# The query-times-key-bias term of plain attention: a row sum on VectorE in place of one-column matmuls

## Chip, cores and metric

One core of one Trainium2 chip. The metric is the device time in microseconds of one execution of the whole program. TensorE runs the matmuls, VectorE (DVE) reductions and elementwise work, ScalarE (ACT) activations, GpSimd (POOL) and SyncE (SP) mostly issue DMAs here.

## What is computed

The program is a stack of four blocks, each with an attention-like and a feed-forward part. The change lies in block 1's attention, "plain attention", over 8 sequences of 112 latent rows with 375 context rows each, all of width 1024:

```python
def _L1_xattn_ref(text, features, Wq, bq, Wk, bk):
    Q = jnp.einsum('btx,dx->btd', text, Wq) + bq
    K = jnp.einsum('bpx,dx->bpd', features, Wk) + bk
    scale = 1.0 / jnp.sqrt(jnp.asarray(K.shape[-1], K.dtype))
    scores = jnp.einsum('btd,bpd->btp', Q, K) * scale
    attn = jax.nn.softmax(scores, axis=-1)
    return jnp.einsum('btp,bpd->btd', attn, features)
...
x = x + jnp.tanh(g_xattn[1]) * _L1_xattn_ref(_layernorm(x, axis=-1), ctx_4096, ...)
```

A score is Q·(features Wk) plus Q·bk. The second term is one number per row of Q, the same for all 375 context rows.

## The kernel before

Plain attention handles the 8 sequences in 4 pairs. PE, VectorE and ScalarE run pairs 0 to 2 in a hardware loop and pair 3 as separate code (`every_pair`, L397). Everything is float32; each matmul of the code becomes two matmul instructions with two weight loads.

TensorE's order in a pair is written out by hand: the query projection of both sequences (L776, `projected("qT", ...)`, into PSUM banks 2, 3, 6, 7), the key projection of Q (L776, `projected("tT", ...)`, banks 0, 1, 4, 5), and then for each sequence s the scores (L792, 8 matmuls of 375 columns) followed by 8 matmuls of one column with the key bias (L795), which put Q·bk into column 400 of the same bank. Then come the transposes of the probabilities of sequence 0 (L807), the transposes of the next pair's normed rows z (L673), those of the probabilities of sequence 1, and the output products (L815).

VectorE does two unlike things. Beside the attention it sorts distances for a nearest-neighbour search that a later block needs: `points.begin` (L500) releases ScalarE's squares, and three sorts per sequence (L521 to L531) follow, each waiting for its squares; the first sort of a sequence also waits until the ranks of the sequence before are stored. Between the sorts of sequence 0 and those of sequence 1 it norms the next pair's rows z in place (L442 to L465). After all sorts it takes up the scores: copy of Q·bk (L915), row maximum (L916), L919 and L921, which release ScalarE's exponential (L870). At the end of a pair it scales the output products and adds them to x (L938).

ScalarE copies qT and tT out of PSUM, does the squares, stores the ranks, takes the norm's roots (in its queue ahead of the squares of sequence 1 and of the copies of tT) and the exponentials. SP loads z of the next pair into the same buffer when its rows have been turned (`zT_ready`), then stores and loads x. POOL loads the biases, the points (a megabyte per sequence, broadcast to all partitions) and the context.

Of the kernel before, what the change touches and what calls it, by code (L numbers as in the profile page):

```python
# [402 lines left out]

def stream_ahead(sp, x, z, x_in, x_out, x_loaded, z_loaded, x_done, x_stored, z_used, at_last):


    for s in range(2):
        sp.dma_start(x[:, s, :], x_in[s]).then_inc(x_loaded[s], 16)

    def pair(p, last):  # L410
        if not last:
            for s in range(2):
                sp.wait_ge(*z_used(s, p))
                sp.dma_start(z[:, s, :], x_in[p * 2 + (s + 2)]).then_inc(z_loaded[s], 16)
        else:
            at_last()
        for s in range(2):

            sp.wait_ge(x_done, p * 2 + (s + 1))
            sp.dma_start(x_out[p * 2 + s], x[:, s, :]).then_inc(x_stored[s], 16)  # L420

            sp.wait_ge(x_stored[s], p * 16 + 16)
            if not last:
                sp.dma_start(x[:, s, :], x_in[p * 2 + (s + 2)]).then_inc(x_loaded[s], 16)

    every_pair(sp, pair)
# [271 lines left out]
def plain_attention(nc, C, banks, gate, x_in, x_out, A, nearest, early, ahead, rise):  # L698
# [4 lines left out]
    with ExitStack() as ctx:  # L703
# [8 lines left out]
        nmax, rsum, coef = (s_.sb(n, [Q, 2, 1]) for n in ("nmax", "rsum", "coef"))  # L712
        qbk, total = s_.sb("qbk", [Q, 2, 1]), s_.sb("total", [Q, 2, 1])
        points = Nearest(s_, [5, 6, 7], 2, nearest, A)
# [8 lines left out]
        max_ready, probs_ready, pT_ready, x_done = (  # L723
            s_.sem(n) for n in ("max_ready", "probs_ready", "pT_ready", "x_done"))

        rows_turned = [(("zT", s, h), 4 * s + h) for s in range(2) for h in range(2)]
        scored = [(("qT", i), (2, 3, 6, 7)[i]) for i in range(4)] + [(("tT", i), (0, 1, 4, 5)[i]) for i in range(4)]
        scored += [((st, s, 0), 4 * s + b0) for st, b0 in (("S", 2), ("pT", 3)) for s in range(2)]
        result = [(("o", s, h), 4 * s + h) for s in range(2) for h in range(2)]
        first = Turns(banks, rows_turned, 1)  # L730
        turns = Turns(banks, scored + rows_turned + result, PAIRS - 1)
        final = Turns(banks, scored + result, 1)
# [3 lines left out]
        def _(sp):  # L736
            def ahead_loads():
# [3 lines left out]
            stream_ahead(sp, x, z, x_in, x_out, x_loaded, z_loaded, x_done, x_stored,  # L741
                         lambda s, p: (zT_ready, p * 2 + (s + 1)), ahead_loads)

        @block.gpsimd
        def _(pool):
            pool.dma_start(bq[:], A["L1_xattn_bq"]).then_inc(b_loaded, 16)
            pool.dma_start(bk[:], A["L1_xattn_bk"]).then_inc(b_loaded, 16)
            with pool.Fori(0, PAIRS) as p:
                for s in range(2):
# [8 lines left out]
        def _(pe):  # L758
            pe.wait_ge(wq_loaded, 16)
            for s in range(2):  # L760
                pe.wait_ge(z_ready, s + 1)
                turn_rows(pe, C, first, z[:, s], "zT", s, 0)

            def pair(p, last):
# [16 lines left out]
                pe.wait_ge(zT_ready, p * 2 + 2)  # L781
                projected("qT", wq, zT, None)
                pe.wait_ge(wk_loaded, 16)
                pe.wait_ge(b_loaded, 32)
                projected("tT", wk, qT, qT_ready)
                for s in range(2):
# [4 lines left out]
                    for k in range(KC):  # L791
                        pe.matmul(now.tile(t)[0:Q, 0:CTX], tT[:, s, k, :], cT[:, s, k, :], start=(k == 0), stop=(k == KC - 1))  # L792

                    for k in range(KC):
                        mm = pe.matmul(now.tile(t)[0:Q, 400:401], qT[:, s, k, :], bk[:, k:k + 1], start=(k == 0),  # L795
                                       stop=(k == KC - 1))
                    mm.then_inc(now.full(t), 1)
# [20 lines left out]

            every_pair(pe, pair)

# [65 lines left out]
        def _(dve):  # L886
            for s in range(2):
                dve.sem_inc(ctx_free[s], 1)
            points.credits(dve)
            norm.in_place(dve, z, z_loaded, 0, z_ready)  # L890

            def pair(p, last):
# [3 lines left out]
                for s in range(2):  # L896
                    for i in range(3):
                        points.sort(dve, p * 2 + s, s, i, (3 * s + i) % 2)
                    if s == 0 and not last:
                        norm.in_place(dve, z, z_loaded, p + 1, z_ready)  # L900
                    if s == 0 and last:
                        for b in range(2):
# [9 lines left out]
                for s in range(2):  # L912
                    t = ("S", s, 0)
                    dve.wait_ge(now.full(t), now.count(t, turn))
                    dve.tensor_copy(qbk[:, s, :], now.tile(t)[0:Q, 400:401])  # L915
                    dve.tensor_reduce(nmax[:, s, :], now.tile(t)[0:Q, 0:CTX], AX, ALU.max, negate=True)  # L916
                    dve.drain()

                    dve.tensor_tensor(total[:, s, :], nmax[:, s, :], qbk[:, s, :], ALU.subtract)  # L919
                    dve.drain()  # L920
                    dve.tensor_scalar(nmax[:, s, :], total[:, s, :], qbk[:, s, :], SCALE, ALU.add, ALU.mult).then_inc(max_ready, 1)  # L921
                for s in range(2):
# [19 lines left out]

            every_pair(dve, pair)

# [2250 lines left out]
def layout(a):  # L3195
# [29 lines left out]
    out["L3_lora_AT"] = out.pop("L3_ffn_lora_A").reshape(512, D).T  # L3225
    out["L3_lora_BT"] = out.pop("L3_ffn_lora_B").transpose(0, 2, 1).reshape(512, D)
    for name in ("L1_xattn_bq", "L1_xattn_bk", "L1_ffn_bu1", "L1_ffn_Wu2"):
        out[name] = a[name].reshape(-1, P).T
# [71 lines left out]
```

## Time and profile before

| what | us |
|---|---|
| median of 3 runs | 2813.17 |
| lowest and highest run | 2810.91, 2819.49 |
| span of the profiled execution | 2820.8 |
| TensorE busy in it | 2583.5 |
| VectorE busy in it | 1907.7 |
| ScalarE busy in it | 1080.2 |

Plain attention takes the stretch from about 968 to 1289 us of the span. The profile shows one execution of the program; busy time counts work, not waiting; the granted clock (PEclk) is TensorE's, 1.00 being 2.4 GHz and 0.50 being 1.2 GHz.

### The profile page before, as it was taken

Reading aid. Unit: us, or ns where it says so; the run is one execution under the profiler, and the core shown is the slowest. Engines: PE = TensorE matmul, PEld = TensorE weight load, DVE = VectorE, ACT = ScalarE, POOL = GpSimd, SP = SyncE. Lnnn points to the kernel's source line nnn. Section 1 sums busy time; section 2 is a strip of 40 time slices with the busy share of each in tenths; the row PEclk is TensorE's granted clock in tenths of the full one; section 3 lists DMA queues with packets and bytes.
Section 4 is the critical chain, followed back from the end, with each engine's and each line's share of the span. In section 5 each row is a group of like instructions: output and inputs, shape, how many; then the busy total and the mean of one; then the engine's idle time right before and its main releaser. Section 6 shows DMA issues by size and latency. Waiting matters only on the chain. (4 is left out here: it accounts for less than half of the span.)

```text
span 2820.8 us, 48283 instructions
## 1 busy us (share of the span) xinstructions
PE 2583.5 (92%) x18264; PEld 1842.1 (65%) x18268; DVE 1907.7 (68%) x3366; ACT 1080.2 (38%) x2605; POOL 564.3 (20%) x602
## 2 busy tenths in 40 slices
PE   7999999999999699998899999998688999868888
PEld 5856855855865388885555555555487788556664
DVE  6376376366467677774578877777558889867774
ACT  3443434334345233332334444443255655302222
POOL 0110100001011300000045454455123334200000
PEclk9999999999999899997899999998799999989999
DMA  8011010111110745556275666544240010544421
GB/s 325 2 38 59 1 59 23 38 35 47 38 60 32 255 112 149 145 160 218 111 238 168 176 172 172 166 133 113 71 186 9 24 46 24 140 143 170 168 96 39
DMA packets 154483, 307.64 MB, mean 109 GB/s; under 512 B 84000, under 2 KB 107200, under 8 KB 144760
## 3 DMA queue, kind: packets, MB, share of 16 engines
q1 hardware_dynamic: 128952, 232.78, 25.6%
q0 software_dynamic: 19376, 57.15, 6.6%
q10 hardware_dynamic: 5936, 14.75, 1.8%
q8 instruction: 141, 2.31, 0.3%
q14 instruction: 78, 0.64, 0.1%
HBM read 249.53 MB, written 42.52 MB: 104 GB/s over the span
## 5 line engine op out<-in xcount | busy, mean ns | idle before, releaser
L1758 DVE TENSOR_REDUCE latent_nmax<-bank 112x1 f32<-112x487 f32 x128 | 85.0, 666 | 242.3 <-PE bank L1561 235.9
L1458 POOL TENSOR_SCALAR latent_probs<-latent_probs,latent_rsum 112x487 f32<-112x487 f32 x128 | 88.1, 688 | 789.6 <-DVE latent_rsum L1763 789.6
L2190 POOL TENSOR_SCALAR grouped_probs<-grouped_probs,grouped_rsum 112x375 f32<-112x375 f32 x256 | 169.6, 680 | 279.4 <-DVE grouped_rsum L2246 279.4
L2457 PE MATMUL bank<-ffn_qT,gather_whole 128*128 128x128 bf16 x3584 | 207.1, 220 | 16.7 <-ACT ffn_us L2580 6.7
L2457 PEld LDWEIGHTS bank<-ffn_qT,gather_whole 128*128 128x128 fp8e4 x3584 | 203.1, 98 | 21.7 <-issue 20.5
L2640 POOL TENSOR_TENSOR ffn_h<-ffn_sl,ffn_us 128x512 f32<-128x512 f32 x56 | 127.4, 2275 | 278.0 <-ACTq L2583 278.0
L2137 ACT ACTIVATE grouped_probs<-bank,grouped_nmax 112x375 f32<-112x375 f32 x256 | 143.3, 573 | 76.4 <-DVE grouped_nmax L2242 76.3
L2242 DVE TENSOR_REDUCE grouped_nmax<-bank 112x1 f32<-112x375 f32 x256 | 122.3, 540 | 72.2 <-PE bank L2048 69.9
L2940 PEld LDWEIGHTS bank<-gather_part,points_onehot 123*128 123x128 bf16 x3072 | 111.9, 103 | 63.1 <-DVE points_onehot L3088 32.6
L2184 POOL TENSOR_SCALAR grouped_raw<-grouped_raw,grouped_rscale 128x1024 f32<-128x1024 f32 x96 | 120.5, 1274 | 144.3 <-DVEq L2220 144.2
L2057 PEld LDWEIGHTS bank<-const_ident,grouped_probs 112*125 112x125 f32 x768 | 105.1, 196 | 67.4 <-DVE grouped_probsT L2254 28.8
L1508 PE MATMUL bank<-latent_zT,front_wq 128*128 128x224 f32 x768 | 148.0, 353 | 0.0
L1533 PE MATMUL bank<-latent_wo,latent_oT 128*128 128x512 f32 x336 | 146.6, 592 | 0.0
L1508 PEld LDWEIGHTS bank<-latent_zT,front_wq 128*128 128x128 f32 x768 | 145.0, 190 | 1.9 <-issue 1.8
L2940 PE MATMUL bank<-gather_part,points_onehot 123*128 123x63 bf16 x3072 | 117.5, 200 | 30.0 <-DVE points_onehot L3088 26.3
L2057 PE MATMUL bank<-const_ident,grouped_probs 112*125 112x112 f32 x768 | 109.8, 282 | 24.8 <-DVE grouped_probsT L2254 18.8
L1468 PE MATMUL bank<-front_wkv,front_cT 128*125 128x384 f32 x384 | 127.0, 491 | 0.0
L1468 PE MATMUL bank<-front_cT,front_wkv 128*128 128x375 f32 x384 | 123.3, 478 | 0.0
L1693 ACT ACTIVATE latent_probs<-bank,latent_nmax 112x487 f32<-112x487 f32 x128 | 85.5, 668 | 89.9 <-DVE latent_nmax L1758 82.4
L2573 ACT ACTIVATE ffn_sl<-ffn_gs,ffn_sgu 128x128 f32<-128x128 f32 x224 | 71.6, 390 | 116.5 <-DVEq L2703 116.1
L1520 PE MATMUL bank<-latent_probsT,latent_v 125*96 125x224 f32 (+1 forms) x512 | 110.2, 358 | 4.1 <-DVEq L1777 4.1
L1533 PEld LDWEIGHTS bank<-latent_wo,latent_oT 128*128 128x128 f32 x336 | 63.2, 190 | 73.9 <-issue 73.7
(435 smaller groups left out, 5576.0 us busy)
## 6 DMA issues: line engine op xcount, KB each, us to landing
grouped_raw<-L_weights SPq DMA_DIRECT2D x24, 2048.0 KB, 9.0
points_spread<-numbers SPq DMA_DIRECT2D x16, 912.0 KB
codes<-grouped_flip SPq DMA_DIRECT2D x24, 512.0 KB, 2.6
front_cT<-ctxT SPq DMA_DIRECT2D x8, 1500.0 KB, 6.8
plain_ctxT<-ctxT POOLq DMA_DIRECT2D x8, 1500.0 KB, 22.5
plain_ctx<-ctx POOLq DMA_DIRECT2D x8, 1500.0 KB, 23.4
grouped_ctx<-ctxT SPq DMA_DIRECT2D x8, 1500.0 KB, 6.7
gather_whole<-numbers SPq DMA_DIRECT2D x12, 912.0 KB
```

The costliest lines, as they stand in the source:

```text
L1468: mm = pe.matmul(turns.tile(t)[0:m, 0:n], lhsT(k), rhs(k), start=(k == 0), stop=(k == KC - 1))
L1508: mm = pe.matmul(turns.tile(t)[:, c * 2 * Q:(c + 1) * 2 * Q], wq[:, k, (2 * i + c) * P:(2 * i + c + 1) * P], zT[:, k].rearrange("p s q -> ...
L1520: mm = pe.matmul(turns.tile(t)[0:HD, 2 * half * Q:2 * (half + 1) * Q], v[0:n, k, g * HD:(g + 1) * HD], pT[0:n, half, k], start=(k == 0), s ...
L1533: mm = pe.matmul(turns.tile(t)[:], oT[:, (b - 1) % 2, k, :], wo[:, k, i * 512:(i + 1) * 512], start=(k == 0), stop=(k == OC - 1))
L2057: mm = pe.transpose(turns.tile(t)[0:CT, j * Q:(j + 1) * Q], pr[:, g % 2, j, k * CT:(k + 1) * CT], C.ident[0:Q, 0:Q])
L2137: act.activation(pr[:, i, j, :], turns.tile(t)[0:Q, 0:CTX], ACT.Exp, bias=nmax[:, i, j:j + 1], accum_out=rsum[:, i, j:j + 1]).then_inc(tur ...
L2184: pool.tensor_scalar(w, w, rscale[:, slot, i % m:i % m + 1], MAGIC, ALU.mult, ALU.add).then_inc(raw_scaled, 1)
L2190: pool.tensor_scalar(pr[:, g % 2, j, :], pr[:, g % 2, j, :], rsum[:, g % 2, j:j + 1], 1.0, ALU.mult, ALU.mult)\
L2242: dve.tensor_reduce(nmax[:, g % 2, j:j + 1], turns.tile(t)[0:Q, 0:CTX], AX, ALU.max, negate=True).then_inc(max_ready, 1)
L2457: mm = pe.matmul(ahead.tile(t)[:, i * P:(i + 1) * P], wgu[:, u0 + f // 4, c:c + 2 * P - 1:2], qT[:, k, :], start=(k == 0), stop=(k == KC - 1))
L2640: pool.tensor_tensor(h[:, G * j:G * j + G, :], sl[:, j % 2], us[:, j % 2], ALU.mult).then_inc(h_ready, 1)
L2940: mm = pe.matmul(turns.tile(t)[:, j * RA:(j + 1) * RA], onehot[0:ROWS, u % 3, j * P:(j + 1) * P], part[n][0:ROWS, b % 2, :], start=(n == 0 ...
```

## The change

Q·bk of a row is z·(Wq bk) + bq·bk, z being the normed row. The vector Wq bk is formed once, at the start of the stage: VectorE multiplies each of the 8 row blocks of Wq with a broadcast row of bk, summing along the row (`tensor_tensor_reduce`), and sums bq times bk. In pair 0, between its two projections, TensorE spreads the result over all partitions by 9 matmuls with the identity, into banks 0, 1 and 4; VectorE reads them after its sorts of sequence 0 (`keys_spread`). From then on, for each pair, VectorE multiplies the normed rows with the spread vector and sums along the row (`summed`), right behind the norm; for pair 0 right behind `keys_spread`. The one-column matmuls L795 and the copy L915 are gone. SP loads the next z only after `summed` has read the old one. The loops of TensorE and VectorE over the pairs are unrolled; those of ScalarE, POOL and SP are kept.

```diff
             for s in range(2):
                 sp.wait_ge(*z_used(s, p))
+                sp.wait_ge(*z_summed(s, p))
                 sp.dma_start(z[:, s, :], x_in[p * 2 + (s + 2)]).then_inc(z_loaded[s], 16)
...
             pool.dma_start(bk[:], A["L1_xattn_bk"]).then_inc(b_loaded, 16)
+            pool.dma_start(key_row, rows(A["L1_xattn_bk_row"], P)).then_inc(key_row_loaded, 16)
...
+            def keys_spread():
+                pe.wait_ge(products_ready, 1)
+                for i in range(3):
+                    t = ("keys", i)
+                    pe.wait_ge(spread.free(t), spread.count(t, 0))
+                    for j in range(4 if i < 2 else 1):
+                        k = 4 * i + j
+                        mm = pe.matmul(spread.tile(t)[0:Q, j * P:(j + 1) * P], key_products[:, k:k + 1].broadcast_to([P, Q]), C.ident[:],
+                                       start=True, stop=True)
+                    mm.then_inc(spread.full(t), 1)
...
                 projected("qT", wq, zT, None)
+                if p == 0:
+                    keys_spread()
                 pe.wait_ge(wk_loaded, 16)
-                pe.wait_ge(b_loaded, 32)
                 projected("tT", wk, qT, qT_ready)
...
                     for k in range(KC):
-                        pe.matmul(now.tile(t)[0:Q, 0:CTX], tT[:, s, k, :], cT[:, s, k, :], start=(k == 0), stop=(k == KC - 1))
-
-                    for k in range(KC):
-                        mm = pe.matmul(now.tile(t)[0:Q, 400:401], qT[:, s, k, :], bk[:, k:k + 1], start=(k == 0),
-                                       stop=(k == KC - 1))
+                        mm = pe.matmul(now.tile(t)[0:Q, 0:CTX], tT[:, s, k, :], cT[:, s, k, :], start=(k == 0), stop=(k == KC - 1))
...
-            every_pair(pe, pair)
+            for p in range(PAIRS):
+                pair(p, p == PAIRS - 1)
...
             norm.in_place(dve, z, z_loaded, 0, z_ready)
+            dve.wait_ge(b_loaded, 32)
+            dve.wait_ge(wq_loaded, 16)
+            dve.wait_ge(key_row_loaded, 16)
+            for k in range(KC):
+                dve.tensor_tensor_reduce(out=row_product, in0=wq[:, k, :], in1=key_row, scale=1.0, scalar=0.0, op0=ALU.mult, op1=ALU.add,
+                                         accum_out=key_products[:, k:k + 1])
+                dve.drain()
+            dve.tensor_tensor(bk[:], bk[:], bq[:], ALU.mult)
+            dve.drain()
+            dve.tensor_reduce(key_products[:, KC:KC + 1], bk[:], AX, ALU.add)
+            dve.drain().then_inc(products_ready, 1)
+
+            def keys_spread():
+                for i in range(3):
+                    t = ("keys", i)
+                    dve.wait_ge(spread.full(t), spread.count(t, 0))
+                    if i < 2:
+                        op = dve.tensor_copy(spread_keys[:, i * 512:(i + 1) * 512], spread.tile(t)[0:Q, :])
+                    else:
+                        op = dve.tensor_reduce(key_products[0:Q, KC + 1:KC + 2], spread.tile(t)[0:Q, 0:P], AX, ALU.add)
+                    op.then_inc(spread.free(t), 1)
+                dve.drain()
+
+            def summed(p):
+                for s in range(2):
+                    dve.tensor_tensor_reduce(out=z_product, in0=z[:, s, :], in1=spread_keys[:], scale=1.0, scalar=0.0, op0=ALU.mult, op1=ALU.add,
+                                             accum_out=qbk[:, p % 2, s, :])
+                    dve.drain()
+                    dve.tensor_tensor(qbk[:, p % 2, s, :], qbk[:, p % 2, s, :], key_products[0:Q, KC + 1:KC + 2], ALU.add).then_inc(qbk_ready, 1)
+                dve.drain()
...
                         points.sort(dve, p * 2 + s, s, i, (3 * s + i) % 2)
+                    if s == 0 and p == 0:
+                        keys_spread()
+                        summed(0)
                     if s == 0 and not last:
                         norm.in_place(dve, z, z_loaded, p + 1, z_ready)
+                        dve.drain()
+                        summed(p + 1)
...
-                    dve.tensor_copy(qbk[:, s, :], now.tile(t)[0:Q, 400:401])
                     dve.tensor_reduce(nmax[:, s, :], now.tile(t)[0:Q, 0:CTX], AX, ALU.max, negate=True)
...
-            every_pair(dve, pair)
+            for p in range(PAIRS):
+                pair(p, p == PAIRS - 1)
```

## Rows read from the trace of the kernel before

**Rows 1.** Pair 1, busy time: start:end, length, each engine, granted clock, DMA, GB/s.
```profile
1058.60:1134.30 75.70, 74.66 (x367) 63.60 (x366) 56.59 (x86) 25.85 (x41) 6.67 (x8) 1.00 0.52 146
```

**Rows 2.** TensorE in order of time, pair 0: start, length, line, operation, count.
```profile
1007.09 24.38 PE L776 MATMUL bank<-plain_qT,plain_wk 128*128 128x224 f32 x128
...
1037.52 1.64 PE L795 MATMUL bank<-plain_bk,plain_qT 128*112 128x1 f32 x16
1039.02 5.29 PE L792 MATMUL bank<-plain_ctxT,plain_tT 128*112 128x375 f32 x16
...
1045.65 0.56 PE L807 MATMUL bank<-const_ident,plain_probs 112*125 112x112 f32 x3
```

**Rows 3.** VectorE in order of time, pair 0; in brackets the idle time before.
```profile
976.08 0.82 DVE L465 TENSOR_SCALAR plain_z<-plain_z,plain_ln_mv 112x1024 f32<-112x1024 f32 x1
980.40 0.18 DVE L500 TENSOR_SCALAR plain_here<-plain_here 128x16 f32<-128x16 f32 x1 [3.50 <-DMA plain_here<-points]
...
984.30 1.23 DVE L521 SCALAR_TENSOR_TENSOR plain_near_far<-plain_near_far 128x1024 f32<-128x1024 f32 x1 [0.22 <-ACT plain_near_far L510]
...
1008.42 1.29 DVE L442 BATCH_NORM_STATS2 plain_ln_stats<-plain_z 112x6 f32<-112x512 f32 x2 [0.40 <-issue]
...
1016.80 1.23 DVE L521 SCALAR_TENSOR_TENSOR plain_near_far<-plain_near_far 128x1024 f32<-128x1024 f32 x1 [2.89 <-DMA nearest<-plain_rank]
...
1040.82 0.16 DVE L915 COPY plain_qbk<-bank 112x1 f32<-112x1 f32 x1 [0.38 <-issue]
```

**Rows 4.** Groups of the stage's instructions: count, busy us and mean ns, idle before.
```profile
L521 DVE SCALAR_TENSOR_TENSOR plain_near_far<-plain_near_far 128x1024 f32<-128x1024 f32 x24 | 29.4, 1225 | 21.7 <-ACT plain_near_far L510 10.5 <-DMA nearest<-plain_rank 8.6 <-issue 2.1
...
L465 DVE TENSOR_SCALAR plain_z<-plain_z,plain_ln_mv 112x1024 f32<-112x1024 f32 x8 | 6.5, 814 | 0.6
...
L927 DVE COPY plain_probsT<-bank 125x336 f32<-125x336 f32 x8 | 4.0, 503 | 2.6 <-PE bank L807 2.6
```

**Rows 5.** The tile z (`plain_z`): its loads from issue to landing.
```profile
DMA to landing us min/median/max: 4.4/11.8/14.4
```

**Rows 6.** TensorE in order of time, pairs 1, 2 and 3.
```profile
1121.37 0.56 PE L807 MATMUL bank<-const_ident,plain_probs 112*125 112x112 f32 x3
...
1124.01 10.46 PE L815 MATMUL bank<-plain_ctx,plain_probsT 125*112 125x512 f32 x24
...
1198.21 0.57 PE L807 MATMUL bank<-const_ident,plain_probs 112*125 112x112 f32 x3 [0.98 <-ACTq L873]
...
1274.95 0.58 PE L807 MATMUL bank<-const_ident,plain_probs 112*125 112x112 f32 x3 [1.05 <-ACTq L873]
...
1276.77 11.69 PE L815 MATMUL bank<-plain_ctx,plain_probsT 125*112 125x512 f32 x24
```

**Rows 7.** VectorE in order of time, pairs 1, 2 and 3.
```profile
1060.30 0.25 DVE L500 TENSOR_SCALAR plain_here<-plain_here 128x16 f32<-128x16 f32 x2 [0.75 <-issue]
...
1118.29 0.16 DVE L915 COPY plain_qbk<-bank 112x1 f32<-112x1 f32 x1 [0.38 <-issue]
...
1172.13 1.23 DVE L521 SCALAR_TENSOR_TENSOR plain_near_far<-plain_near_far 128x1024 f32<-128x1024 f32 x1 [2.69 <-DMA nearest<-plain_rank]
...
1196.14 0.16 DVE L915 COPY plain_qbk<-bank 112x1 f32<-112x1 f32 x1 [0.38 <-issue]
...
1212.53 0.25 DVE L500 TENSOR_SCALAR plain_here<-plain_here 128x16 f32<-128x16 f32 x2 [0.40 <-issue]
...
1214.96 1.23 DVE L521 SCALAR_TENSOR_TENSOR plain_near_far<-plain_near_far 128x1024 f32<-128x1024 f32 x1 [2.18 <-ACT plain_near_far L510]
...
1238.78 1.29 DVE L138 BATCH_NORM_STATS2 mem_stats<-mem_x 128x6 f32<-128x512 f32 x2 [0.30 <-issue]
```

**Rows 8.** Three short stretches: columns as in the first group.
```profile
976.00:986.00 10.00, 9.22 (x33) 8.40 (x34) 2.80 (x5) 5.65 (x7) 2.68 (x3) 0.52 1.01 352
...
1020.00:1024.00 4.00, 4.00 (x23) 4.00 (x22) 3.85 (x6) 0.01 (x1) 0.00 (x0) 1.00 0.32 133
...
1276.00:1278.00 2.00, 2.00 (x5) 1.39 (x6) 1.09 (x5) 0.00 (x0) 0.00 (x0) 0.50 0.06 12
```

More of the change, by code:

```diff
@@ L401, in every_pair, with stream_ahead @@
     pair(PAIRS - 1, True)
-def stream_ahead(sp, x, z, x_in, x_out, x_loaded, z_loaded, x_done, x_stored, z_used, at_last):
+def stream_ahead(sp, x, z, x_in, x_out, x_loaded, z_loaded, x_done, x_stored, z_used, at_last, z_summed):
     for s in range(2):
@@ L712, in plain_attention @@
         nmax, rsum, coef = (s_.sb(n, [Q, 2, 1]) for n in ("nmax", "rsum", "coef"))
-        qbk, total = s_.sb("qbk", [Q, 2, 1]), s_.sb("total", [Q, 2, 1])
+        qbk, total = s_.sb("qbk", [Q, 2, 2, 1]), s_.sb("total", [Q, 2, 1])
+        spread_keys, key_products = s_.sb("spread_keys", [Q, D]), s_.sb("key_products", [P, KC + 2])
+        flat_t, flat_p = tT[:].rearrange("p s k q -> p (s k q)"), pr[:].rearrange("q s n -> q (s n)")
+        key_row, row_product, z_product = flat_t[:, 0:D], flat_t[:, D:D + D // 2].bitcast(BF16), flat_p[:, 0:D // 2].bitcast(BF16)
         points = Nearest(s_, [5, 6, 7], 2, nearest, A)
@@ L724, in plain_attention @@
             s_.sem(n) for n in ("max_ready", "probs_ready", "pT_ready", "x_done"))
+        key_row_loaded, products_ready, qbk_ready = (s_.sem(n) for n in ("key_row_loaded", "products_ready", "qbk_ready"))
         rows_turned = [(("zT", s, h), 4 * s + h) for s in range(2) for h in range(2)]
@@ L730, in plain_attention @@
         first = Turns(banks, rows_turned, 1)
+        spread = Turns(banks, [(("keys", i), (0, 1, 4)[i]) for i in range(3)], 1)
         turns = Turns(banks, scored + rows_turned + result, PAIRS - 1)
@@ L741, in _ @@
             stream_ahead(sp, x, z, x_in, x_out, x_loaded, z_loaded, x_done, x_stored,
-                         lambda s, p: (zT_ready, p * 2 + (s + 1)), ahead_loads)
+                         lambda s, p: (zT_ready, p * 2 + (s + 1)), ahead_loads, lambda s, p: (qbk_ready, p * 2 + (s + 1)))
         @block.gpsimd
@@ L914, in pair @@
                     dve.wait_ge(now.full(t), now.count(t, turn))
-                    dve.tensor_copy(qbk[:, s, :], now.tile(t)[0:Q, 400:401])
                     dve.tensor_reduce(nmax[:, s, :], now.tile(t)[0:Q, 0:CTX], AX, ALU.max, negate=True)
                     dve.drain()
-                    dve.tensor_tensor(total[:, s, :], nmax[:, s, :], qbk[:, s, :], ALU.subtract)
+                    dve.tensor_tensor(total[:, s, :], nmax[:, s, :], qbk[:, p % 2, s, :], ALU.subtract)
                     dve.drain()
-                    dve.tensor_scalar(nmax[:, s, :], total[:, s, :], qbk[:, s, :], SCALE, ALU.add, ALU.mult).then_inc(max_ready, 1)
+                    dve.tensor_scalar(nmax[:, s, :], total[:, s, :], qbk[:, p % 2, s, :], SCALE, ALU.add, ALU.mult).then_inc(max_ready, 1)
                 for s in range(2):
@@ L3226, in layout @@
     out["L3_lora_BT"] = out.pop("L3_ffn_lora_B").transpose(0, 2, 1).reshape(512, D)
+    out["L1_xattn_bk_row"] = a["L1_xattn_bk"]
     for name in ("L1_xattn_bq", "L1_xattn_bk", "L1_ffn_bu1", "L1_ffn_Wu2"):
```

## The prediction, made before the kernel was run
> **What bounds the kernel now.** I read the trace in this order: the grouped stretches of the plain-attention stage, then TensorE's order of time, then VectorE's, then the costs of single operations.
>
> One pair of the stage lasts 75.70 us, and TensorE has work in 74.66 of them, VectorE in 56.59 [rows 1]. That looks like a stage bound by TensorE, with a quarter of VectorE's time to spare. The order of time says otherwise. In pair 0 TensorE finishes the second score block (its last one-column products included) and starts the first transposes of the probabilities at 1045.65 without a pause [rows 2], while VectorE reaches its first work on the scores (L915) only at 1040.82, straight from sorting [rows 3]. The road from there to these transposes is the copy, the maximum, two small operations and ScalarE's exponential. Pair 2 gives its length: VectorE starts at 1196.14 [rows 7] and TensorE, having waited 0.98 us, starts at 1198.21 [rows 6], so 2.07 us. By that, pair 0 could not have transposed before 1042.89, a slack of 2.8 us against 1045.65; pair 1 (1118.29 + 2.07 = 1120.36 against 1121.37, [rows 6, 7]) has 1.0 us; pairs 2 and 3 have none, since TensorE itself waits about 1 us there (0.98 and 1.05, [rows 6]). So both engines are bounds, within 3 us of each other in every pair. VectorE's idle time lies elsewhere: behind ScalarE's squares at the head of a pair, behind a store of ranks, and beside the output products.
>
> **What the change removes.** Eight one-column products per sequence, run as 16 instructions. In pair 0 they begin at 1037.52 and the next score block begins at 1039.02 [rows 2], so 1.50 us per sequence, 3.0 per pair, 12.0 in all. All of it lies on TensorE ahead of the transposes. VectorE's one-column copy L915 goes too, from the road of 2.07 us: it overlaps its successor but for 0.08 us, an estimate from half of a small operation. Since VectorE arrives later than, or within 2.8 us of, the transposes, little of the 12.0 can be cashed unless VectorE also gets earlier.
>
> **What it adds on VectorE.** The new multiply-and-sum over 1024 columns isn't in the trace. Nearest rows: a two-input operation on 128x1024 float numbers takes 1.225 us and a one-input one 0.814 us [rows 4]. I take 1.30, the two-input row and a drain, with 0.85 as the lower bound; 1.5 would be it with a small operation of 0.2 for writing out the sum. Once per kernel come 8 of them and two tiny operations with drains: 10.4 + 0.45 = 10.9 us. Once, in pair 0, come the three reads of PSUM after the sorts of sequence 0: the copy of 125x336 took 0.503 [rows 4], so two of 512 columns and one sum of 128 cost some 1.6 us. Per pair (`summed`) there are two long operations and two adds, 2.95 us. It runs twice in pair 0 (for pairs 0 and 1), once in pairs 1 and 2, never in pair 3.
>
> As a rule beside this: the Trainium skill, Vector Engine (DVE) Microarchitecture Reference, section 7 ("Points that are easy to get wrong"), says that an operation of the scalar-tensor-tensor family with two SBUF sources that aren't bf16 runs at half rate, as no port is left for reading back the accumulator. By that the new operation would take twice its price, and the sum would be that of the first rival below. The 1.225 us row speaks against it for a plain two-input operation, but no row has the accumulator.
>
> **Pair 0, step by step.** Before, VectorE ended the norm at about 976.9, waited for the points (until 980.40) and for ScalarE's first squares, and sorted from 984.30 [rows 3]. Now the products stand in between. They need the broadcast key row, whose load is queued on POOL ahead of the points: it lands no earlier than VectorE is free (976.9) and hardly later than the much longer load that was there at 980.40; I take 978.7, the middle. The products end at 978.7 + 10.9 = 989.6. Only then does `points.begin` release ScalarE's squares, which take 3.9 us to the sort as before (980.40 to 984.30). The sort starts at 993.4, 9.1 us late: the old idle time isn't filled, it comes again behind the products. The three sorts end near 1017.0.
>
> TensorE meanwhile ends the query projection at 1007.09 [rows 2] and runs 18 spreading instructions, at 0.10 us (the one-column pace) to 0.19 (24.38/128 of the projection), 1.8 to 3.4 us. Then it stops: the key projection needs bank 0, which VectorE empties only after its three sorts. So it restarts at about 1017.7, 10.6 us late, of which 7 to 9 are idle. VectorE goes on: three reads 1.6, `summed(0)` 2.95, to 1021.6. The next rows z are now loaded only when `summed` has read the old ones (SP's new wait), at 1020.2 and 1021.6, no longer when the first rows are turned. Such loads took 4.4 us at least, 11.8 in the median, 14.4 at most [rows 5]; the DMA share was 1.01 where the first ones ran, while this stretch showed 0.32 [rows 8] and the next points' megabyte will join, so I take 6.0, near the minimum. The second z lands at 1027.7. Behind it lie its statistics and both scalings, 3.8 of the norm's 5.5 us (1008.42 to 1016.80 less 2.89, [rows 3]). So a wait of 4.4 us is new, the norm ends at 1031.5, `summed(1)` at 1034.5. ScalarE's two roots, the squares and the key projection's copies are queued behind the same statistics, but have time. The wait of 2.89 us for the rank store [rows 3] vanishes beneath this, and the unrolled code gives a little: three sorts with their gaps took 24.12 us in the loop (984.30 to 1008.42, [rows 3]) and 23.82 in the unrolled last pair (1214.96 to 1238.78, [rows 7]), so 0.3 per sequence.
>
> The sum for VectorE: 9.1 + 1.6 + 2.95 + 4.4 + 2.95 - 2.89 - 0.6 = +17.5 us, so it reaches the scores at 1058.3, and the transposes start at 1058.3 + 2.07 - 0.08 = 1060.3 against 1045.65: **+14.6 us**. TensorE alone would be ready sooner: from the key projection's start to the end of both score blocks took 1007.09 to 1042.65 (1045.65 less two times 1.50 of one-column products), so 1017.7 + 35.6 = 1053.3. After its idle time the clock may start at half, as in 976 to 986 (0.52, [rows 8]), which costs up to 5 us more; 1058.3 is still covered.
>
> **Pairs 1 to 3.** Pair 1: `summed` +2.95; unrolling -0.6 for two sequences and -0.35 at the pair's head (VectorE's gap before L500 is 0.75 in the loop, 0.40 in the last pair, [rows 7]); copy -0.08. VectorE is 1.9 later, the slack was 1.0: +0.9. Pair 2: the same +1.9, but the wait of 2.69 for the rank store [rows 7] stands right behind `summed` and hides most of it: -0.8. Pair 3 has only the lost copy, -0.1. Together 0.
>
> **The clock.** Where TensorE waited ahead of the last pair's transposes, after 1.6 us of sparse one-column work, its granted clock went from 1.00 to 0.50 [rows 8], that is 2.4 to 1.2 GHz, and the output products took 11.69 us instead of 10.46 [rows 6]; with the slower transposes about 1.6 us. Pair 2's wait of 0.98 cost nothing. Now the waits there are 2.5 to 4 us in pairs 0 to 2. I take half of three times 1.6: +2.4, with 0 and 4.8 as ends.
>
> **Sum.** 14.6 + 0 - 0.1 + 2.4 = +16.9 us. The profiled execution's span of 2820.8 becomes 2837.7. It stands 7.6 us above the median of the runs, 2813.17, from which I forecast 2830. The ends: a z load at its median of 11.8 adds 5.8; sums at 1.5 us add 2.4 in pair 0 and 0.8 later; the clock 2.4. Short loads (z 4.4, key row at once) take 3.3 off, no clock loss 2.4.
>
> **Rivals.** *Half-rate sums*: each long operation 1.23 us longer, 12 of them on VectorE's road in pair 0 (14.7) and two in each of pairs 1 and 2 (4.9): 2830 + 19.6 = 2850. For it, the price that no row shows; against it, the 1.225 row. Chance 0.12. *Cheap sums and loads*: at 0.85, 12 x 0.45 = 5.4 less, with a z load of 4.4 us and no clock loss 4.0 less: 2821, the edge of what counts as a change. Chance 0.12. *TensorE cashes its 12.0 us*: VectorE's additions fall into its idle time and TensorE sets every pair, 2801. The place is pair 0's road to 1045.65; for it speaks VectorE's quarter of idle time, and it decides from the point where pair 0's 14.6 is gone, which needs sums of 1.30 - 14.6/12 = 0.1 us, or of 0.45 with a z load that costs no wait. No row is near that. Chance 0.05. That the change doesn't do what it says, I see no way to: the products and the copy are gone from the code.
>
> **How the numbers follow.** The forecast (2823 to 2842 with its own ends) has 0.71. The range 2821 to 2850 leaves out the faster case and the tail of the half-rate one. About 0.3% (8.4 us) is what a measurement of this kernel can tell from no change: slower 0.85, within 0.10 (most of the cheap case), faster 0.05.
>
> **What would show it.** Right, if the trace after has pair 0 some 15 us longer and the others within 1 us; if TensorE stands idle for 7 to 9 us between the spreading and the key projection, released by VectorE's copy; if the first sort begins near 993; if VectorE waits for a z load before pair 0's second norm; if the new operation takes near 1.25 us. Wrong, if the sums take below 0.9 or above 2 us, if the key row lands past 981, or if pair 1 or 2 moves by over 3 us.

## The result, and the profile after

The changed kernel takes 2835.8 us (median of 8 runs) against 2818.95 (8 runs of the kernel before); the ratio is 1.0079, interval 1.0060 to 1.0097. The forecast of slower, 2830 in 2821 to 2850, held. The two medians lie 16.9 us apart; the interval of the ratio stands for 17 to 27 us, so the whole kernel's time can't tell the forecast +16.9 from somewhat more.

The profiled executions differ by less than the stage does: the spans are 2832.3 and 2820.8, 11.5 us apart, but behind the stage the kernel before took 9.6 us longer in that one execution (1526.95 us from the next stage's first transposes to the end, against 1517.4), in code that the change doesn't touch. So the stage alone is compared from here on, from TensorE's first turned rows to the first transposes of the next stage: 317.82 us before, 338.56 after, **+20.7**. By pair, from one query projection to the next (pair 3: to the end of its output products):

| pair | before | forecast of the difference, without the clock | after | difference | of it, transposes to end of output products |
|---|---|---|---|---|---|
| 0 | 78.60 | +14.6 | 94.79 | +16.2 | +1.3 |
| 1 | 75.72 | +0.9 | 78.54 | +2.8 | +2.1 |
| 2 | 76.85 | -0.8 | 78.52 | +1.7 | +2.1 |
| 3 | 77.29 | -0.1 | 77.41 | +0.1 | +0.3 |

The +20.7 holds for these two executions. In pair 0 the query projection took 27.26 us before and 24.48 after:

```profile
980.00 27.26 PE L776 MATMUL bank<-plain_zT,plain_wq 128*128 128x224 f32 x128 [0.75 <-ACTq L684]
```

In the later pairs it takes 24.38 in both kernels. How long the clock stays low at the start of this projection differs between executions: it took 27.2 to 27.35 us in nine of the thirteen traces of this case and 24.48 in the other four. Before, TensorE set pair 0 and the slow start counts; after, VectorE sets it and the start doesn't count. With a fast start before, the difference would be some 23 us (an estimate, 20.7 + 2.8).

TensorE in order of time, changed kernel (start, length, line, operation; in brackets the idle time before and what ended it; lines are numbered 1 to 50 higher than before):

```profile
980.25 24.48 PE L794 MATMUL bank<-plain_zT,plain_wq 128*128 128x224 f32 x128 [0.67 <-ACTq L685]
1004.56 2.13 PE L778 MATMUL bank<-const_ident,plain_key_products 128*112 128x128 f32 x18
1019.64 26.69 PE L794 MATMUL bank<-plain_qT,plain_wk 128*128 128x224 f32 x128 [12.95 <-issue]
...
1060.79 0.58 PE L822 MATMUL bank<-const_ident,plain_probs 112*125 112x112 f32 x3 [3.35 <-ACTq L889]
...
1138.51 0.97 PE L822 MATMUL bank<-const_ident,plain_probs 112*125 112x112 f32 x3 [3.80 <-ACTq L889]
...
1142.89 10.85 PE L830 MATMUL bank<-plain_ctx,plain_probsT 125*112 125x512 f32 x24
...
1217.05 0.97 PE L822 MATMUL bank<-const_ident,plain_probs 112*125 112x112 f32 x3 [3.79 <-ACTq L889]
...
1295.67 1.95 PE L822 MATMUL bank<-const_ident,plain_probs 112*125 112x112 f32 x6 [3.89 <-ACTq L889]
```

The first three lines answer to the first of [rows 2]: between the projections stand 18 spreading instructions, and TensorE then stops for 12.95 us. The transposes, which in pairs 0 and 1 came without a pause [rows 2, 6], now wait 3.4 to 3.9 us in all four pairs. Without the one-column matmuls TensorE is ready earlier, and VectorE isn't.

VectorE in order of time, changed kernel:

```profile
979.99 1.22 DVE L911 CUSTOM_DVE_ANT_0 plain_tT<-plain_wq,plain_tT 128x1024 bf16<-128x1024 f32 x1 [2.40 <-DMA plain_tT<-L_xattn_bk_row]
981.14 0.08 DVE L911 DVE_READ_ACCUMULATOR2_ANT plain_key_products<- 128x1 f32 x1
...
991.25 0.25 DVE L501 TENSOR_SCALAR plain_here<-plain_here 128x16 f32<-128x16 f32 x2
995.04 1.23 DVE L522 SCALAR_TENSOR_TENSOR plain_near_far<-plain_near_far 128x1024 f32<-128x1024 f32 x1 [3.54 <-ACT plain_near_far L511]
...
1018.85 1.29 DVE L924 COPY plain_spread_keys<-bank 112x512 f32<-112x512 f32 x2 [0.30 <-issue]
...
1026.15 1.29 DVE L443 BATCH_NORM_STATS2 plain_ln_stats<-plain_z 112x6 f32<-112x512 f32 x2 [2.83 <-DMA plain_z<-x]
...
1058.87 0.55 DVE L966 TENSOR_REDUCE plain_nmax<-bank 112x1 f32<-112x375 f32 x1 [0.31 <-issue]
```

Against [rows 3]: the release of the squares moved from 980.40 to 991.25, the first sort from 984.30 to 995.04, the scores from 1040.82 to 1058.87. The new operation shows as a custom operation of 1.22 us and a read of the accumulator of 0.08; one follows the next after 1.35 us.

Two short stretches around pair 1's transposes, changed kernel (columns as in the first group of rows):

```profile
1136.00:1138.00 2.00, 0.00 (x0) 0.00 (x0) 1.54 (x5) 0.30 (x1) 0.95 (x2) 0.71 0.00 0
1138.00:1140.00 2.00, 1.49 (x7) 1.49 (x8) 1.04 (x5) 0.36 (x2) 0.11 (x1) 0.50 0.88 311
```

In pair 1 the granted clock goes from 1.00 to 0.50 while TensorE waits for VectorE, and the transposes behind the wait run at 1.2 GHz. In pair 0 it fell a little later: the first three transposes still took 0.58 us there.

### The profile page after: what moved, and what is told of

Its sections match the earlier page's. It is cut to its first block and busy times, and to the rows that moved or that the text cites. A ratio compares the mean times of both kernels' runs of the same rounds, so it can differ in the third digit from the quotient of the medians.

```text
span 2832.3 us, 48030 instructions
## 1 busy us (share of the span) xinstructions
PE 2574.4 (91%) x18154; PEld 1831.5 (65%) x18158; DVE 1931.0 (68%) x3403; ACT 1079.4 (38%) x2605; POOL 564.7 (20%) x603
## 5 line engine op out<-in xcount | busy, mean ns | idle before, releaser
L794 PE MATMUL bank<-plain_qT,plain_wk 128*128 128x224 f32 x512 | 99.8, 358 | 13.0 <-issue 13.0
```

## The experiments

Times are of the stage, cut as above, in one profiled execution each, unless a ratio is given. The one kernel that was traced twice (all rearrangements together, below) came to 320.0 and 317.2 us: its pairs 1 and 2 agreed within 0.2 us, its pairs 0 and 3 differed by 1.6 and 1.4. So a stage difference below 3 us shows nothing by itself, and the order of time within the pairs has to carry the reading.

**Removal alone.** The first question is what the 12.0 us of one-column matmuls were worth.

```diff
                     for k in range(KC):
-                        pe.matmul(now.tile(t)[0:Q, 0:CTX], tT[:, s, k, :], cT[:, s, k, :], start=(k == 0), stop=(k == KC - 1))
-
-                    for k in range(KC):
-                        mm = pe.matmul(now.tile(t)[0:Q, 400:401], qT[:, s, k, :], bk[:, k:k + 1], start=(k == 0),
-                                       stop=(k == KC - 1))
+                        mm = pe.matmul(now.tile(t)[0:Q, 0:CTX], tT[:, s, k, :], cT[:, s, k, :], start=(k == 0), stop=(k == KC - 1))
...
-                    dve.tensor_copy(qbk[:, s, :], now.tile(t)[0:Q, 400:401])
...
-                    dve.tensor_tensor(total[:, s, :], nmax[:, s, :], qbk[:, s, :], ALU.subtract)
-                    dve.drain()
-                    dve.tensor_scalar(nmax[:, s, :], total[:, s, :], qbk[:, s, :], SCALE, ALU.add, ALU.mult).then_inc(max_ready, 1)
+                    dve.tensor_scalar(nmax[:, s, :], nmax[:, s, :], SCALE, None, ALU.mult).then_inc(max_ready, 1)
```

> The kernel before with the one-column matmuls, the copy L915 and L919 left out: the term Q·bk, one number per row, isn't computed (the softmax over a row doesn't depend on it). The stage's length is counted from TensorE's first turned rows to the first transposes of the next stage: 317.8 us in the trace before. Theory (VectorE sets the stage, TensorE's slack behind it is small): of TensorE's 12.0 us only the slacks come back, 2.8 in pair 0, 1.0 in pair 1, some 0.3 in each of pairs 2 and 3 from the missing small operations, so at most -4.4; and as TensorE now waits longer ahead of the transposes, the clock may fall there and take 1.5 to 2.1 back in each of pairs 0 to 2. Stage 313.4 to 318.6. Rival (TensorE sets the stage): -12, stage 305.8.

Measured: 313.97, 3.9 less. TensorE, kernel without the products:

```profile
1041.08 0.57 PE L803 MATMUL bank<-const_ident,plain_probs 112*125 112x112 f32 x3 [0.44 <-ACTq L869]
...
1115.42 0.57 PE L803 MATMUL bank<-const_ident,plain_probs 112*125 112x112 f32 x3 [1.52 <-ACTq L869]
...
1191.62 0.89 PE L803 MATMUL bank<-const_ident,plain_probs 112*125 112x112 f32 x3 [3.38 <-ACTq L869]
```

TensorE waits in every pair now: it ran into VectorE, as the slacks of 2.8 and 1.0 us said. Pair 0 is 2.5 us shorter, pair 1 1.4, pair 3 0.6, and pair 2 is 0.6 longer: behind its wait of 3.38 us the transposes are slow (0.89 instead of 0.57). The rival's -12 is out. So even with nothing put in their place, the removed matmuls are worth a third of their own time. The 2.5 us of pair 0 rest on the slow start of its query projection (27.26 before, 27.20 here), which is where its slack came from.

**Unrolling alone.**

```diff
-            every_pair(pe, pair)
+            for p in range(PAIRS):
+                pair(p, p == PAIRS - 1)
```

and the same on VectorE.

> The kernel before with the loops of TensorE and VectorE over the pairs unrolled, as the change does, and nothing else. Theory: VectorE is 0.9 us earlier in each of pairs 0 to 2 (0.3 per sequence, 0.35 at a pair's head); pairs 0 and 1 don't show it, since TensorE sets them, pair 2 does: stage 317.8 - 0.9 = 316.9. Rival: the longer code costs something by itself (its loading stands in the way), so that a part of the +20.7 us of the changed kernel comes from here: stage 320 or more.

Measured: 316.65, 1.2 less; pairs 0 and 1 are 0.1 and 0.2 shorter, pair 2 1.3, and pair 3 is 0.5 longer. The longer code costs nothing that shows, and none of the +20.7 comes from it.

**Filling TensorE's wait.**

```diff
+                    if s == 0:
+                        pe.wait_ge(now.free(("pT", 0, 0)), now.count(("pT", 0, 0), turn))
+                        for k in range(5):
+                            pe.matmul(now.tile(("pT", 0, 0))[0:Q, 0:CTX], tT[:, 1, k, :], cT[:, 1, k, :], start=(k == 0), stop=(k == 4))
                     t = ("pT", s, 0)
                     pe.wait_ge(probs_ready, p * 2 + (s + 1))
```

> The changed kernel with five useless score matmuls per pair (of 375 columns, 10 instructions, 3.2 us) in TensorE's wait ahead of the transposes of the probabilities, into the bank that the transposes then overwrite. Theory (the clock): the granted clock stays at 1.00 there in every pair, from the first transposes to the output products it takes 2.6 us again instead of 3.5, 4.4 and 4.4, and these 10.5 instead of 10.9: stage 338.6 to 333, though TensorE does more. Rival (the waits on the other engines make these steps slow, or the clock falls anyway): no change, 338.6, or up to 1 us longer where the useless work outlasts the wait.

Measured: 331.05, 7.5 less than the changed kernel, with more work in it. TensorE, pair 1 of the filled kernel, and a stretch of it (columns as in the first group of rows):

```profile
1130.86 3.32 PE L821 MATMUL bank<-plain_ctxT,plain_tT 128*112 128x375 f32 x10
1134.81 0.58 PE L826 MATMUL bank<-const_ident,plain_probs 112*125 112x112 f32 x3 [0.63 <-ACTq L893]
...
1137.47 10.46 PE L834 MATMUL bank<-plain_ctx,plain_probsT 125*112 125x512 f32 x24
```

```profile
1134.00:1138.00 4.00, 3.23 (x25) 2.59 (x25) 2.06 (x8) 2.50 (x7) 0.40 (x1) 1.00 0.76 264
```

The granted clock stays at 1.00 here, the transposes take 0.58 instead of 0.97, and the output products begin 2.66 us behind them instead of 4.38 and take 10.46 instead of 10.85. Pairs 1, 2 and 3 are 2.1 us shorter each, pair 0 1.2. This is the clock, shown by the same code with the wait filled. I had left pair 3 out of the expectation, which had paid for a slow clock, some 1.6 us, before the change already [rows 6, 8].

**TensorE's stop.**

```diff
                     for i in range(3):
                         points.sort(dve, p * 2 + s, s, i, (3 * s + i) % 2)
+                        if s == 0 and p == 0 and i == 1:
+                            keys_spread()
                     if s == 0 and p == 0:
-                        keys_spread()
                         summed(0)
```

> The changed kernel, VectorE reading the spread vector out of PSUM after the second sort of pair 0 instead of after the third: TensorE's stop ahead of the key projection, 12.95 us, ends 7.9 us earlier. Theory (VectorE's own chain sets pair 0, the stop lies beside it): TensorE's stop falls to about 5 us, VectorE reaches the scores at the same time, the stage stays within 0.5 of 338.6. Rival (the stop is what pair 0 lost): up to 8 us shorter, 330.6.

Measured: 337.85, 0.7 less. TensorE:

```profile
1010.95 24.45 PE L794 MATMUL bank<-plain_qT,plain_wk 128*128 128x224 f32 x128 [2.18 <-issue]
1047.77 13.21 PE L811 MATMUL bank<-plain_ctxT,plain_tT 128*112 128x375 f32 x32 [12.37 <-ACTq L882]
```

TensorE's stop ahead of the key projection went from 12.95 to 2.18 us, and pair 0 got no shorter (95.6 against 94.8). The time is spent waiting further down, 12.37 us for ScalarE's copies of the key projection, which stand in its queue behind the roots and squares that wait for VectorE. The stop lies beside the chain, and the rival's 8 us are out. But VectorE didn't reach the scores at the same time, as expected: counted from the stage's start it came 2.1 us later (84.6 against 82.5), since its wait for z was 5.14 us instead of 3.08. The loads of z were issued at the same point, but the third sort, which frees the buffer of the next points, ended later, so their megabyte was issued 1.7 us later, closer to the loads of z. That this made them slower is read from the trace, not tested. In all, pair 0 is 0.8 longer, and pairs 1 and 2 are 0.8 shorter each (77.7 instead of 78.5), where the clock fell for a shorter time.

**The loads of z.**

```diff
                         if s == 0 and p == 0 and i == 1:
                             keys_spread()
+                            summed(0)
-                    if s == 0 and p == 0:
-                        summed(0)
```

(against the kernel of the experiment before)

> The changed kernel, VectorE reading the spread vector and summing pair 0's rows (which frees the buffer of z) after the second sort of pair 0 instead of after the third. Theory (the loads of z are on the chain that sets pair 0): they are issued 7.9 us earlier and land beneath the third sort, VectorE's waits of 2.83 and 0.25 us for them vanish, and the stage goes from 338.6 to 335.5, give or take 1 us for the clock. Rival (the loads lie beside the chain): no change, 338.6.

Measured: 334.20, 4.4 less; pair 0 alone is 91.61, 3.2 less. The wait for z is gone from VectorE's rows:

```profile
1020.69 1.28 DVE L443 BATCH_NORM_STATS2 plain_ln_stats<-plain_z 112x6 f32<-112x512 f32 x2 [0.30 <-issue]
```

The loads were on the chain, at 3.1 us as read from the trace. The rest comes from pairs 1 and 2 (0.7 and 0.8 less), where the clock fell for a shorter time; pair 3 is 0.3 longer.

**ScalarE's squares beside the products.**

```diff
                                          accum_out=key_products[:, k:k + 1])
                 dve.drain()
+                if k in (3, 5):
+                    points.begin(dve, k // 5, k // 5, 0)
...
                 for s in range(2):
-                    points.begin(dve, p * 2 + s, s, p)
+                    if p > 0:
+                        points.begin(dve, p * 2 + s, s, p)
```

> The changed kernel, the two small operations that release ScalarE's squares in pair 0 standing behind the fourth and the sixth of the eight products with the rows of Wq instead of behind all of them. Theory (the products push a serial step, release, squares, sort, ahead of them): ScalarE's squares run beside the products, the wait of 3.54 us ahead of the first sort vanishes, the first sort begins right behind the products, and the stage goes from 338.6 to 335.0. Rival (pair 0 is set by TensorE's late key projection): under 1 us shorter. If the points haven't landed by the fourth product, the gain is smaller by that wait.

Measured: 337.88, 0.7 less: a miss. VectorE, and a stretch of the same kernel:

```profile
990.55 1.22 DVE L522 SCALAR_TENSOR_TENSOR plain_near_far<-plain_near_far 128x1024 f32<-128x1024 f32 x1 [0.20 <-issue]
...
1025.64 1.29 DVE L443 BATCH_NORM_STATS2 plain_ln_stats<-plain_z 112x6 f32<-112x512 f32 x2 [6.82 <-DMA plain_z<-x]
```

```profile
1020.00:1022.00 2.00, 2.00 (x13) 2.00 (x12) 0.00 (x0) 0.00 (x0) 0.00 (x0) 1.00 0.99 310
1022.00:1024.00 2.00, 2.00 (x12) 2.00 (x12) 0.00 (x0) 0.00 (x0) 0.00 (x0) 1.00 1.00 243
```

The first half came true: the wait ahead of the sort fell from 3.54 to 0.20, and counted from the stage's start the sort begins 3.6 us earlier (15.05 against 18.68). The gain is eaten by the next wait, 6.82 us for z instead of 3.08. The loads were issued 3.6 us earlier as well, but took 8.0 us to land instead of 4.0. The points' megabyte, issued 2.8 us ahead of them as in the changed kernel, now ran beside the tail of the context loads and took 6.7 us to land instead of 4.8; between 1018 and 1020 us its queue had the whole DMA share (1.03) and z moved nothing. From then on z met a share of 0.99 to 1.00. The changed kernel's loads met 0.96 to 1.00 too, so the full share alone isn't the reason; that the longer load ahead of them is, no run tests. Counted from the stage's start z landed at 50.1 us, in the changed kernel at 49.8. Pair 0 stayed at 94.79. So the two waits have to be taken away together, which the run with all rearrangements does.

**Row sums twice.**

```diff
                         norm.in_place(dve, z, z_loaded, p + 1, z_ready)
                         dve.drain()
+                        if p > 0:
+                            summed_again(p + 1)
                         summed(p + 1)
```

(`summed_again` is the two long operations of `summed` with their drains, without the adds)

> The changed kernel with each row sum of pairs 1 and 2 done twice (four more long operations of 1.30 us in all, with drains). Theory (VectorE sets these pairs, and nothing covers its row sums): each of the two pairs becomes 2.6 to 2.7 us longer, the stage goes from 338.6 to 344.0. Rival (the sums fall into idle time and only the clock makes the pairs longer): no change, 338.6.

Measured: 339.03, 0.5 more; pairs 1 and 2 are 0.6 longer each, not 2.7. At first sight the rival's case. VectorE and TensorE of that kernel, pair 1:

```profile
1137.96 0.55 DVE L974 TENSOR_REDUCE plain_nmax<-bank 112x1 f32<-112x375 f32 x1 [0.31 <-issue]
```

```profile
1073.70 24.38 PE L794 MATMUL bank<-plain_zT,plain_wq 128*128 128x224 f32 x128
...
1125.53 12.05 PE L811 MATMUL bank<-plain_ctxT,plain_tT 128*112 128x375 f32 x32 [3.23 <-ACTq L882]
1139.88 0.58 PE L822 MATMUL bank<-const_ident,plain_probs 112*125 112x112 f32 x3 [2.31 <-ACTq L889]
1142.55 10.46 PE L830 MATMUL bank<-plain_ctx,plain_probsT 125*112 125x512 f32 x24
```

```profile
1125.00:1127.00 2.00, 1.47 (x3) 0.89 (x4) 2.00 (x3) 1.72 (x3) 0.00 (x0) 0.71 0.03 8
1140.00:1142.00 2.00, 2.00 (x19) 1.79 (x19) 0.81 (x4) 1.10 (x3) 0.00 (x0) 1.00 0.86 352
```

VectorE reaches the scores 64.26 us into the pair (1073.70 to 1137.96); in the changed kernel it is 61.55 (1075.04 to 1136.59). That is +2.7, just the price: nothing covers the row sums. But VectorE's delay also holds up ScalarE's copies, TensorE's wait is split, 3.23 us ahead of the scores and 2.31 ahead of the transposes, and the clock falls at the first of them (0.71 at the start of the scores, 1.00 at the transposes): the score matmuls take 12.05 instead of 10.36, which is hidden, and the transposes and output products are fast again, 2.67 us and 10.46. So 2.7 us of work and 2.1 us of clock cancel. The theory on VectorE stands; my expectation left the clock where it was.

**All rearrangements together.** The edits for the loads of z and for the squares, and in each pair

```diff
                 dve.drain()
+                if not last:
+                    for s in range(2):
+                        points.begin(dve, p * 2 + (s + 2), s, p + 1)
                 for s in range(2):
                     dve.wait_ge(x_loaded[s], p * 16 + 16)
```

in place of the release at the head of pairs 1 to 3.

> The changed kernel with both rearrangements of pair 0 (release of the squares amid the products, reading and summing after the second sort), and in each pair the release of the next pair's squares ahead of the output products instead of behind them. Theory: pair 0 is 6.7 us shorter; in pairs 1 to 3 VectorE no longer waits 3.5 us (2.2 in pair 3) for the squares, TensorE hardly waits ahead of the transposes, so the clock stays at 1.00 there and 1.7 to 2.1 us more come back in each: stage 338.6 to about 317, as long as that of the kernel before (317.8). Rival (another wait, the points' loads or the rank stores, takes the place of the squares'): 325 or more.

Measured: 320.0, 18.5 less than the changed kernel, 3 us short of the theory's 317 and well below the rival's 325. TensorE:

```profile
1068.30 24.38 PE L794 MATMUL bank<-plain_zT,plain_wq 128*128 128x224 f32 x128
...
1128.34 0.58 PE L822 MATMUL bank<-const_ident,plain_probs 112*125 112x112 f32 x3 [0.36 <-ACTq L889]
...
1141.31 24.38 PE L794 MATMUL bank<-plain_zT,plain_wq 128*128 128x224 f32 x128
```

Pair 0 is 6.4 us shorter (88.4), pairs 1 and 2 take 73.0 and 72.7, 3 us less than the 75.7 of [rows 1]: with VectorE out of the way, TensorE's 3.0 us per pair come back. Pair 3 gained only 0.9, where the theory had some 4. Of pair 0's loss 9.8 us remain. VectorE's added work there is 11.3 us of products (979.99 to 991.25), 1.6 of reads and 5.7 of sums, part of it in time that was idle before; no run leaves any of it out, so this part is read from the order of time and not tested. Timed on its own:

> The rearranged changed kernel of the run before with this edit, timed. Theory: the stage of 320.0 against 317.8 says +2 us, which this measurement can't tell from no change; per pair it saves 3 us behind pair 0 and loses 10 in it. Rival: the one run that came out 5 us below the kernel before on the same chip was no accident, ratio below 0.998.

Ratio 0.9999 (0.9983 to 1.0015), stage 317.2: no change against the kernel before, as the stage said. What it saves in pairs 1 to 3 (2.7, 4.0 and 2.2 us) it loses in pair 0 (8.3).

**The early release alone,** on the kernel before (unrolled), with its one-column matmuls:

> The kernel before with the loops of TensorE and VectorE unrolled and the release of the next pair's squares standing ahead of the output products instead of behind them; the one-column matmuls stay. Theory (both engines set the stage, within 3 us): VectorE gets 3.5 us earlier per pair, but TensorE's own work then sets all pairs: pairs 0 and 1 as in the unrolled kernel (78.5 and 75.6), pair 2 the same, pair 3 loses its wait of 1.4 and its slow clock of 1.7: stage 316.7 - 3.1 = 313.6, some 4 us below the kernel before. Rival (VectorE sets the stage alone): 3.5 us less in each of three pairs, 306.

Measured: 311.70, ratio 0.9978 (0.9966 to 0.9991), 0.2% faster than the kernel before; the interval just excludes no change. The traced execution was the fastest of its ten. TensorE:

```profile
980.18 24.48 PE L776 MATMUL bank<-plain_zT,plain_wq 128*128 128x224 f32 x128 [0.67 <-ACTq L684]
...
1269.65 0.58 PE L807 MATMUL bank<-const_ident,plain_probs 112*125 112x112 f32 x3
...
1272.12 10.47 PE L815 MATMUL bank<-plain_ctx,plain_probsT 125*112 125x512 f32 x24
```

Pairs 1 and 2 are TensorE's own 75.55; pair 3's first transposes come without a wait, and its output products take 10.47. Pair 0 was 75.65 rather than 78.5, since the clock rose earlier in its query projection (24.48 us instead of 27.3), which differs between runs of the same code (27.35 and 24.48 in the two traces of the rearranged kernel); without these 2.9 us the stage would be 314.6, within 1 of the expectation. The rival's 306 is out: TensorE bounds these pairs.

**Early release and no products.**

> As the run before, and the one-column matmuls, the copy and L919 left out too: Q·bk isn't computed, one number per row, on which a softmax doesn't depend. Theory: with both engines eased, TensorE's 12.0 us come back at last: pair 0 -2.8, pairs 1 to 3 about -3 each against the kernel before them, stage 313.6 - 12 = 302. Rival (VectorE's other waits, for the rank stores, 2 to 3 us in pairs 0, 2 and 3, take over): 306 to 308.

Measured: 306.34, ratio 0.9942 (0.9918 to 0.9967). Pairs 0 to 2 take 75.4, 72.4 and 72.4, against the unrolled kernel's 78.5, 75.55 and 75.55: TensorE's 3.2 us each come back. Pair 3 gained nothing (82.3 from its query projection to the next stage's transposes, 81.1 in the run before). VectorE there:

```profile
1228.30 1.29 DVE L138 BATCH_NORM_STATS2 mem_stats<-mem_x 128x6 f32<-128x512 f32 x2 [1.28 <-DMA mem_x<-x]
...
1232.46 1.23 DVE L521 SCALAR_TENSOR_TENSOR plain_near_far<-plain_near_far 128x1024 f32<-128x1024 f32 x1 [2.35 <-ACT plain_near_far L510]
```

In pair 3 VectorE also norms the next stage's rows; it waited 1.58 us in all for their loads and then 2.35 for ScalarE's squares, and TensorE waited 2.48 us, with a slow clock behind it. So the theory's 302 was missed in pair 3, which took 76.9 us where the run before less 3.2 would be 72.5, and the rival's 306 came by other waits than the rank stores that it named.

## Why the prediction was right, and where it was off

**VectorE's price per operation**: right. 1.35 us from one product to the next against 1.30; `summed` took 2.85 us against 2.95; the three reads of PSUM 1.6, as forecast. The half-rate rival falls: 1.225 us for 1024 columns, the duration of the two-input row [rows 4]. By the rule of the Trainium skill (Vector Engine (DVE) Microarchitecture Reference, section 7) it would have run at half rate, with two float32 sources in SBUF and an accumulator; the trace doesn't agree, and the measurement decides. The profile names the new operation a custom one, and no run shows whether the rule's family includes it.

**Pair 0's chain**: right in its steps. The key row was in place at 979.99 against 978.7 (the stage began 0.3 later); the first sort came at 995.04 against 993.4; the wait for z was 3.1 against 4.4, as the loads took 4.0 us and not 6.0; VectorE reached the scores at 1058.87 against 1058.3, the transposes came at 1060.79 against 1060.3. That the end agrees so closely is luck in part: the first sort was 1.3 us late by the stage's own start, the wait for z was 1.3 short, and the two cancel. That the idle time ahead of the first sort wouldn't absorb the products but come again behind them shows as 3.54 us [rows 3: 3.50 and 0.22 before, for the points and the squares]. TensorE's stop was 12.95 us instead of 7 to 9, since its query projection ran 2.8 us faster and VectorE's reads came 1.9 later than forecast; it is not on the chain, as the early read showed. The profile doesn't name what ended the stop; TensorE restarts 0.8 us after VectorE's first copy begins (1018.85 to 1019.64), and it did so in the early read too (1010.16 to 1010.95).

**Pair 0's slack** of 2.8 us was read rightly, but not where it came from: it is the slow start of that execution's query projection, 27.26 us instead of 24.48. A fast start takes 2.8 us off, and the slack would be gone (an estimate, 2.8 less 2.8). The +14.6 is counted from the slow one.

**Pairs 1 to 3 without the clock**: +0.7, -0.4 and -0.2 against +0.9, -0.8 and -0.1. With it they are +2.8, +1.7 and +0.1, so the sign that pairs 1 and 2 stay within 1 us didn't come, and pair 1 came near the 3 us named as a sign of being wrong. In pair 2 the wait of 2.69 us for the rank store is gone, hidden by `summed`.

**The clock**: the term that was mis-sized. I took half of three times 1.6, +2.4, with 4.8 as the upper end; it came to 1.3 + 2.1 + 2.1 + 0.3 = 5.8 us. The granted clock fell at the transposes of all four pairs, not of half of three, and at 2.1 us in pairs 1 and 2, because there the slow stretch also covers the transposes of the next rows, which the last pair, the source of my 1.6, doesn't have. The 3.4 us of this and 0.4 elsewhere are the difference between +16.9 and the stage's +20.7. So the agreement of the medians' 16.9 us with the forecast 16.9 is luck: the traced stage moved by 3.8 us more, and the rest of the program differs by as much between executions (9.6 us in these two). The ends listed under the prediction's sum give some 2824 and 2841 rather than 2823 and 2842; nothing hangs on it.

What stays open: whether the clock falls at a given wait. Waits of 3.4 to 3.9 us were followed by 0.50 in the changed kernel, one of 1.52 wasn't in the kernel without products, but pair 3 of the kernel before fell after 1.05 us of waiting behind sparse matmuls, where its pair 2, with 0.98 us behind the same matmuls, didn't; and the split waits of 3.2 and 2.3 fell only at the first. In pair 0 of the rearranged kernels a wait of 1.95 us was followed by slow transposes (the loads of z) and one of 1.57 wasn't (all rearrangements, second trace). I can price it from the rows around it; I couldn't have said which pairs.

## What to carry to other kernels

An engine that is busy in 74.66 of 75.70 us may still have another engine one microsecond behind it: before moving work from the busy one, read from the order of time by how much the other is early at the point where they meet, since no more than that comes back. Work that a change does once still has to fit in a pass in which nothing is idle: count what is released only behind it, such as another engine's first step or the reload of a buffer. Where TensorE is made to wait, price its clock behind the wait too; here that was 5.8 of 20.7 us, and useless matmuls in the wait gave 7.5 back, some 1.6 of them in the last pair, which had been slow before the change too. And before reading a slack from one trace, look whether it stands on something that differs between executions, as the start of pair 0's query projection does here.

## What the runs showed of the hardware that I hadn't expected

Filling a wait of 3.4 to 3.9 us with 3.3 us of useless matmuls made the stage 7.5 us shorter, as the clock then stayed at 1.00. Adding 2.7 us to VectorE's chain in a pair made that pair only 0.6 longer, because the added wait moved the fall of the clock to matmuls that another wait hid. Loads of 448 KB issued 3.6 us earlier landed no earlier, 8.0 us after their issue instead of 4.0, behind a megabyte that itself took 6.7 us instead of 4.8. And the first query projection of the stage took 24.48 us in four traces and 27.2 to 27.35 in nine; the one kernel that was traced twice shows one of each.
